# Moving two rank events, one exponential, the routing weights and the halves of a matrix product in the first stage of a transformer-and-experts kernel

## What is computed

```
q = (x @ Wq).reshape(B, L, H, d)
feat = elu(q) + 1.0
KV = einsum('nshd,nshv->nhdv', feat, q / L);  Ksum = feat.sum(axis=1)
Z = 1.0 / (einsum('nlhd,nhd->nlh', feat, Ksum) + 1e-6)
msg = einsum('nlhd,nhdv,nlh->nlhv', feat, KV, Z) * L
msg = msg.reshape(B, L, D) @ Wm
x1 = x + _layernorm(msg, g1, b1)
mlp = relu(msg @ W1) @ W2
x1 = x1 + _layernorm(mlp, g2, b2)
x1 = _layernorm(x + x1)
logits = x1 @ router_w.T
probs = softmax(logits);  topk_w, topk_ids = top_k(probs, 8)
topk_w = topk_w / topk_w.sum()
pos = rank of each token among those that chose the same expert
```

## Time and profile before

| | |
|---|---|
| median of 3 runs | 648.25 us (645.24 to 648.62) |
| profiled execution | 652.67 us |
| span of its trace | 650.7 us |
| PE busy | 562.6 us (86%) |
| DVE busy | 462.1 us (71%) |
| POOL busy | 427.9 us (66%) |
| ACT busy | 305.8 us (47%) |
| first stage, by PE | from 4 us to 137 us of the span |

### The profile page before, as it was taken

The page is one execution under the profiler, slowest core; times in us unless marked ns, Lnnn a source line. Parts: engine busy times, 40 slices in busy tenths (PEclk is TensorE's granted clock), DMA queues, the critical chain, the costliest instruction groups (busy, mean ns, idle before and its releaser), DMA issues.

```text
span 650.7 us, 10440 instructions
## 1 busy us (share of the span) xinstructions
PE 562.6 (86%) x3231; PEld 459.8 (71%) x3231; DVE 462.1 (71%) x1568; ACT 305.8 (47%) x825; POOL 427.9 (66%) x471
## 2 busy tenths in 40 slices
PE   5889888899238877999899999999999999999993
PEld 4678777855226655787687887878878788788762
DVE  1577877789949423576677879778787787886873
ACT  3667756449201111225364736636456365463440
POOL 5453422319574576538887988979979799753673
PEclk9999989799555555579999999999999999999998
DMA  4688455789320121142330030300302100000000
GB/s 130 170 229 316 186 218 196 313 255 233 80 73 28 47 61 50 37 170 99 127 131 2 8 138 9 135 4 10 138 9 93 46 9 9 2 17 0 10 8 17
DMA packets 47225, 62.04 MB, mean 95 GB/s; under 512 B 13026, under 2 KB 39873, under 8 KB 46146
## 3 DMA queue, kind: packets, MB, share of 16 engines
q1 hardware_dynamic: 44610, 56.15, 26.8%
q0 software_dynamic: 2560, 5.23, 2.8%
HBM read 35.16 MB, written 24.13 MB: 91 GB/s over the span
## 4 chain that ended last, share of the span: by engine, by line
PE 59%; DVE 19%; issue 6%; ACT 6%; POOL 3%; DMA 3%; another core or an unknown queue 2%; SPq 1%; POOLq 0%; DVEq 0%; ACTq 0%
PE pair L1446 8%; PE pair L1448 8%; PE pair L1447 8%; PE pair L1779 5%; DVE c_g L1247 2%; PE pair L602 2%; PE pair L628 2%; PE pair L1558 2%; DVE cand L1975 2%; PE pair L1494 2%; PE pair L1789 2%; PE pair L1568 2%; PE pair L555 2%; POOL c_acc L959 2%
## 5 line engine op out<-in xcount | busy, mean ns | idle before, releaser
L959 POOL TENSOR_TENSOR c_acc<-c_acc,c_g 128x512 f32<-128x512 f32 x112 | 144.6, 1291 | 37.6 <-DVE c_g L1247 30.0
L1095 ACT ACTIVATE c_sg<-pair 128x256 f32<-128x256 f32 x256 | 95.3, 385 | 93.3 <-PE pair L1448 90.4
L1247 DVE SCALAR_TENSOR_TENSOR c_g<-pair,c_comb,c_sg 128x256 f32<-128x256 f32 x224 | 100.4, 478 | 27.0 <-ACT c_sg L1095 22.7
L1446 PE MATMUL pair<-c_w_hi,c_x3h 128*128 128x512 f32 x256 | 108.9, 426 | 12.2 <-DVE c_g L1247 11.3
L1448 PE MATMUL pair<-c_w_hi,c_x3l 128*128 128x512 f32 x256 | 101.0, 395 | 0.0
L1447 PE MATMUL pair<-c_w_lo,c_x3h 128*128 128x512 f32 x256 | 100.7, 393 | 0.0
L1446 PEld LDWEIGHTS pair<-c_w_hi,c_x3h 128*128 128x128 f32 x256 | 48.2, 188 | 23.5 <-DVE c_g L1247 14.2
L1448 PEld LDWEIGHTS pair<-c_w_hi,c_x3l 128*128 128x128 f32 x256 | 48.0, 188 | 11.2
L1447 PEld LDWEIGHTS pair<-c_w_lo,c_x3h 128*128 128x128 f32 x256 | 48.3, 189 | 8.0
L1857 POOL DMA_INDIRECT routed_rows<-x1T_all,dest_row x32 | 31.7, 992 | 28.9 <-DVE x1T_all L1769 21.2
L1852 POOL DMA_INDIRECT rows_all<-token_rows,tok_row x32 | 31.3, 978 | 14.8 <-issue 9.4
(11 more groups left out here) (374 smaller groups left out, 1489.3 us busy)
## 6 DMA issues: line engine op xcount, KB each, us to landing
routed_rows<-rows_all SPq DMA_DIRECT2D x8, 2048.0 KB
c_c<-routed_rows SPq DMA_DIRECT2D x7, 2048.0 KB, 7.8
token_rows<-a_xw SPq DMA_DIRECT2D x8, 384.0 KB, 2.8
a_x<-in_L_attn_x SPq DMA_DIRECT2D x8, 256.0 KB, 3.0
base_all<-a_xw SPq DMA_DIRECT2D x8, 256.0 KB, 3.5
c_c<-routed_rows SPq DMA_DIRECT2D x4, 512.0 KB, 5.2
out<-c_outb SPq DMA_DIRECT2D x16, 128.0 KB, 1.8
wgu_late<-in_L_ffn_w_gate SPq DMA_DIRECT2D x4, 480.0 KB, 7.7
```

Of the source, the lines that this page charges most:

```text
L959: g.tensor_tensor(acc, acc, b["g"][:, (2 * uf + i) % 4, :, :], ALU.add).then_inc(s["acc"], 1)
L1095: a_.activation(b[f"sg{q % 2}"][:, x, :], self.pair[q % 2][:, x, H1:2 * H1], SIG).then_inc(s["sig"], 1)
L1247: v.scalar_tensor_tensor(out=dst, in0=self.pair[q % 2][:, x, 0:H1], scalar=b[f"comb{uf}"][:, j * E1 + e:j * E1 + e + 1], in1=b[f"sg{q % 2} ...
L1446: t.matmul(dst, w_hi, x_hi, start=start, stop=False)
```

## The change

1. **Events.** Events 0 and 1 both stand in step 7, the last sequence's step. Step 6 becomes a full step like those before it. To have both in one step, event 0 uses banks 1 and 2, event 1 uses banks 0 and 6, with new waits: the first half of `hT` in step 8 for both `keyT` writes, event 1's products for `msg_sb`, and the fillers of step 7 for both copies of `maskT`.
2. **Halves.** The first half of W1's product goes to bank 6, the second to bank 5. Only the second half waits for the copy of the logits.
3. **Exponential.** On ACT, L303 stands ahead of the copy of `msgT` in steps where the next q is made early.
4. **Routing weights.** On DVE, L509, L511 and L515 stand ahead of L497 to L504.
5. **Fillers.** 4 rather than 6 in a step; the 20 of step 9 stay.

```diff
-    EVENTS = {6: (0,), 7: (1,), B + 2: (2, 3)}
+    EVENTS = {7: (0, 1), B + 2: (2, 3)}
...
-                a.activation(b["hT"][:, 0, :], bank[5][:, :], ACT.Relu).then_inc(s["hT_sb"], 1)
+                a.activation(b["hT"][:, 0, :], bank[6][:, :], ACT.Relu).then_inc(s["hT_sb"], 1)
                 act.wait_ge(s["hT_mm"], 2 * n + 2)
-                a.activation(b["hT"][:, 1, :], bank[6][:, :], ACT.Relu).then_inc(s["hT_sb"], 1)
+                a.activation(b["hT"][:, 1, :], bank[5][:, :], ACT.Relu).then_inc(s["hT_sb"], 1)
...
-                a.copy(b["maskT"][:, i % 2, :], bank[0 if i == 3 else 1][:, :]).then_inc(s["maskT_sb"], 1)
+                a.copy(b["maskT"][:, i % 2, :], bank[1 - i % 2][:, :]).then_inc(s["maskT_sb"], 1)
...
+            if self.ahead(k + 1):
+                exponential(k + 1)
...
-                exponential(k + 1)
+                    exponential(k + 1)
...
-            if k < self.N and k in self.EVENTS:
-                self.write_keys(dve, self.EVENTS[k][0])
+            if k < self.N:
+                for i in self.EVENTS.get(k, ()):
+                    self.write_keys(dve, i)
...
                 pe.wait_ge(s["msgT_sb"], n + 1)
+                if n == self.N - 1:
+                    pe.wait_ge(s["key_sb"], 2)
...
-                if n >= 2:
-                    pe.wait_ge(s["lg_sb"], n - 1)
                 for h in range(2):
-                    t.matmul(bank[5 + h][:, :], b["WmW1"][:, h * D:(h + 1) * D], b["msgT"][:, :], start=True, stop=True).then_inc(s["hT_mm"], 1)
+                    if h and n >= 2:
+                        pe.wait_ge(s["lg_sb"], n - 1)
+                    t.matmul(bank[6 - h][:, :], b["WmW1"][:, h * D:(h + 1) * D], b["msgT"][:, :], start=True, stop=True).then_inc(s["hT_mm"], 1)
...
-                unread(20 if n == self.N - 1 else 6, bank[0])
+                if k in self.EVENTS and k < self.N:
+                    pe.wait_ge(s["maskT_sb"], 2)
+                unread(20 if n == self.N - 1 else 4, bank[0])
...
-                    pe.wait_ge(s["key_sb"], 1)
-                rank = bank[6 if i == 3 else 2]
+                    pe.wait_ge(s["msg_sb"], k + 1)
+                rank = bank[6 if i % 2 else 2]
```

More of the change, by code:

```diff
@@ L491, in dve @@
                 v.tensor_tensor(by_half(ex), by_half(ex), mask, ALU.mult).then_inc(s["pick"], 1)
+            if 0 <= m < self.N:
+                dve.wait_ge(s["pick"], 5 * m + 3)
+                v.tensor_reduce(b["esum"][:, :], ex, AX.X, ALU.add).then_inc(s["pick"], 1)
+                dve.wait_ge(s["pick"], 5 * m + 4)
+                v.reciprocal(b["esum"][:, :], b["esum"][:, :]).then_inc(s["pick"], 1)
+                dve.wait_ge(s["pick"], 5 * m + 5)
+                if m >= 2:
+                    dve.wait_ge(self.xw_stored[m % 2], 32 * (m // 2))
+                v.tensor_tensor(b[f"xw{m % 2}"][:, :, D:ROW], ex, bcast_last(b["esum"][:, :], E0), ALU.mult).then_inc(s["w_sb"], 1)
             n = k
@@ L506, in dve @@
                 ins.then_inc(s["msg_sb"], 1)
[L507 to L515, removed]
             n = k - 1
@@ L546, in write_keys @@
         at = h * 2 * L + part * L
-        v.scalar_tensor_tensor(out=self.keyT[:, at:at + L], in0=bank[6 if i == 3 else 2][:, :], scalar=b["offs"][:, part:part + 1],
+        v.scalar_tensor_tensor(out=self.keyT[:, at:at + L], in0=bank[6 if i % 2 else 2][:, :], scalar=b["offs"][:, part:part + 1],
                                in1=b["maskT"][:, h, :].bitcast(F32), op0=ALU.add, op1=ALU.mult).then_inc(s["key_sb"], 1)
@@ L636, in pe @@
                     pe.wait_ge(s["featT_sb"], k + 1)
-                transposes(bank[0 if i == 3 else 1], lambda j: b["mask"][:, part, j, h, :, :].rearrange("p u e -> p (u e)")).then_inc(s["maskT_mm"], 1)
+                transposes(bank[1 - i % 2], lambda j: b["mask"][:, part, j, h, :, :].rearrange("p u e -> p (u e)")).then_inc(s["maskT_mm"], 1)
             n = k
```

## The result

| | before | changed |
|---|---|---|
| median of 20 runs each, same chip | 649.61 us | 646.24 us |
| lowest and highest | 645.24, 653.08 us | 642.46, 650.08 us |
| ratio, 95% interval | | 0.9951 (0.9928 to 0.9973) |
| profiled execution, span | 652.67, 650.7 us | 650.08, 648.1 us |

The change is faster by 3.4 us (0.5%; 1.8 to 4.7 by the interval) where 5.45 (0.84%) was forecast. The time of 646.24 lies just inside the range of 640.8 to 646.5, but by size the forecast missed: taken from the median of 20 runs before, 649.61, it would have said 644.2. The profiled execution of the changed kernel took 650.08 us, the longest of its 20 runs. It shows well what can go wrong, and it is not a typical execution.

What follows compares the result with a forecast made beforehand. A chain across engines, no engine being full, was taken to set the step. Terms: -3.0 + 0.3 + 0 + 0 - 4.85 + 2.1 = -5.45 us, taking 648.25 to 642.8; range (8 in 10) 640.8 to 646.5.

Steps and rivals of the forecast that it cites:

- Turns: Ends of steps 2 to 5: W1's first half no longer waits for the logits' copy, 0.75 us each, -3.0 us.
- Early steps: Steps 0 and 1: the early exponential delays step 0's path; step 1's delay is covered by the feat wait; +0.3 us once.
- Fillers and weights: Full steps: two fillers less only lengthen PE's wait for x1; the weights fill DVE's wait for num; 0 us each.
- the 646.3 that has a chance of 0.04: Outcome in the prediction's spread of chances: 646.3 us, chance 0.04.
- Step 6: Becomes a full step without its event: 12.13 us instead of 16.98, -4.85 us.
- Step 7: Takes both events, with a 2.1 us wait for the mask copies: 14.4 us instead of 12.28, +2.1 us.
- the rival at 0.25: The clock falls in step 7's new wait: one fall costs 1.7 us, so -3.7 and 644.5 us; chance 0.25.
- The rest of the kernel: Stages behind the first, from keyT in step 10: assumed to let the whole gain through.
- The second rival: Median executions had no slow stretch in step 6: 1.7 us of gain missing, some tenths spilled; about 646.2 us; chance 0.12.
- the first rival: The clock falls in step 7's new wait, one fall costing 1.7 us: 644.5 us; chance 0.25.

Runs made afterwards that it cites:

- e4: Kernel before with only the halves of W1's product swapped and the logits' wait on the second half: 627.71 us, ratio 0.9904.
- e10: Changed kernel with 6 fillers in a step instead of 4: 643.95 us, ratio 0.9939 to the kernel before.
- e12: Kernel before with halves swapped, weights moved and exponential early from step 2; events in steps 6 and 7, 6 fillers: 643.30 us, ratio 0.9918.
- e3: Kernel before with both events in step 7, with their banks and waits, and nothing else: 634.06 us, ratio 1.0004.
- e7: Kernel before with only the routing weights moved ahead of z and msg on DVE: 632.17 us, ratio 0.9985.
- f3: Further profiled execution of the kernel before, nothing changed, on a third chip: 636.65 us.
- f4: Second further profiled execution of the kernel before, nothing changed, on a third chip: 632.41 us.
- e2: Changed kernel with eight more unread products ahead of step 7's wait for both maskT copies: 626.95 us, ratio 0.9883 to the kernel before.
- e1: Changed kernel timed once more, nothing altered, beside the kernel before: 632.00 us, ratio 0.9959.

## Why the forecast was right and where it was not

**Turns, -3.0 forecast.** Right in mechanism, a little small: 0.92 each, -3.7 for four. The halves alone give 0.85 (e4). The other 0.07 are the two fillers less: with six of them a full step takes 12.03 us in e10, and in e12 too, which has the early exponential. Beside the swapped halves the exponential adds nothing to a full step. I took 0.75, with an allowance of my own for a semaphore between, which no row shows; L607 starts 0.84 after L692, whose row takes 1.00, and 0.84 was the upper end.

**What the turns were also worth.** This was missing. e4 gave 6.6 us (4.4 to 7.9 by its interval), while the steps of its profile give about 5.0 against those of the kernel before without a fall: 3.4 in steps 2 to 5, 1.35 in step 6, 0.3 in step 7. With the wait at the turn went the falls behind it, one or two of 1.7 us in three of three profiled executions of the kernel before (none in those of e3 and e7, which have the same turns). That these falls are the missing 1.6 fits the sizes and was not tested by itself. I read one of them in the earlier trace rows and treated it as a matter of step 6.

**Early steps, +0.3.** 0.27 in step 0, and 0.27 in step 1 that the wait for `feat` covered (0.74 before, 0.47 after). The rest of the +1.24 in the table is not the change's: products between 14.6 and 16.3 us took twice their time, and the same stands in f3, an execution of the kernel before. Their cause stays open, since the granted clock reads 1.00 there. Of step 2's -1.72 some 0.5 is such a piece too: 14.37 with PE waiting 0.30 us for a load of x, 13.88 in other profiles of the kernel before.

**Fillers and weights, 0.** Nearly right: the fillers gave 0.07 in a full step, and the weights nothing there, with the 2.13 us of L530 as worked out. What they give in a step with an event (0.38, e7) the working did not see, and the changed kernel has no use for it. POOL went first in each full step, by 0.06 to 0.07 us (in step 4 L262 at 65.24, L532 at 65.31, to 67.44):

```profile
65.24 1.26 POOL L262 TENSOR_TENSOR a_r<-a_x,a_b 128x512 f32<-128x512 f32 x1
...
65.31 2.13 DVE L532 SCALAR_TENSOR_TENSOR a_r<-a_gm,a_rstd,a_r 128x128 f32<-128x128 f32 x4 [0.33 <-POOL a_rstd L254]
```

No run shows the 646.3 that has a chance of 0.04 in the prediction, a delay of POOL's addition by DVE's: the additions stood in this order in all full steps.

**Step 6, -4.85.** This term was mis-sized. It set a length of 16.98, with a fall in it, against one without. Without a fall step 6 took 15.29 (f4), so the term was -3.3 (15.29 to 11.96). Of that 1.35 comes from the halves alone (e4: 13.94), and 2.0 is left for the events' move. The working had said itself that 1.7 of the term hung on the fall. That this 1.7 was not missing in the end is luck: one or two such falls went with the waits at the turns, which the sum had not counted there.

**Step 7, +2.1.** Measured +2.06 (14.34) when the clock is kept, by the steps that were worked out: wait 1.91 for 2.1, end at 14.34 for 14.4. So beside the halves the events' move makes steps 6 and 7 longer by 0.34 us (11.96 + 14.34 against 13.94 + 12.02 in e4), a small loss. The two terms had booked a gain of 2.75.

**The clock in the new wait.** This is the step that failed. The term of step 7 let the clock stay up through a new wait of 2 us, so the sum had the fall at nothing, and the rival at 0.25 priced it at 1.7. Step 7 lost 3.25 (17.59 against 14.34) and step 8 to the end 1.3 more (26.90 against 25.6) in the profiled execution. e2 against e1 puts the filled wait at 5.05 us in the median. I had taken the length of a fall from the earlier trace rows, where it lasted for about one L602: that took 3.59 us, and from 82.5 to 86.1 us the mean granted clock was 0.53. Here it lasted 10 us. What is not shown is how many executions have this fall: none of the three profiles of the changed kernel on the faster chips does, and there the account rests on e2's median.

**The sum again.** Turns -3.7, start +0.3, step 6 -3.3, step 7 +2.1 give -4.6. One or two falls that the turns lose add -1.7 to -3.4: -6.3 to -8.0. The changed kernel with its wait filled (e2) measured -7.3 (5.6 to 9.2 by its interval), so without the fall in the new wait the gain is larger than the 5.45 of the forecast. That fall gives back the 5.05 of e2 against e1 and leaves -1.3 to -3.0. Measured were 2.3 (e1) and, on the first chip, 3.4.

**The rest of the kernel** let the gain through, as assumed, on the faster chip: 493.7 to 495.3 us from the first stage's end in eight kernels. In the six profiles from the slower sets it took 510.2 to 513.5 us, so there a part of every difference between single executions comes from behind the stage.

**The rivals' sums.** Two do not come out of their own terms. The second rival takes back 1.7 us and "some tenths", which makes 644.5 and a little more, not 646.2. The forecast's own range of 641.3 to 644.3 is wider than the bounds of its terms, which add up to about 642.1 to 643.8. That the measured 646.24 stands beside the 646.2 of the second rival and inside the range is chance: what happened is the first rival, at a higher price.

## What to carry to other kernels

Before a change is priced against a profile, its slow-clock stretches have to be taken out of the terms, or priced by their own: a fall in the one execution shown can be missing from the next (three profiles of the kernel before had theirs at the start of step 6, of steps 4 and 6, and of step 5). A new wait of PE can cost more than its own length: behind the one of 1.91 us the granted clock was 0.50 for 10 us in one profile of the changed kernel, and stayed at 1.00 in three others. If it can't be avoided, put work into the wait, which cost nothing on the path here (14.34 us with and without, e2 and e1); work behind it showed no gain (e10). And test a bundle part by part: here one part, the swap of two banks with its later wait (e4), was worth more than the whole (e1).

## What the runs showed of the hardware

The granted clock fell to 0.50 behind waits of only 0.68 and 0.72 us (before, f3, f4), and in steps 3 to 9 it stayed low between some 3.4 us (e10) and 10 us (the changed kernel), the latter with PE busy without a gap. A DVE instruction (L515) that started 0.16 us after POOL's addition did (L262, at 93.38 us in the kernel before) took 1.39 us, against 0.43 in step 4. The kernel before took 649.0 and 649.6 us in two sets and 632 to 634 us in the three others, which ran on other chips. Full steps had the same length on all of them (11.95 to 11.97 in the changed kernel), and the difference lies behind the first stage: about 512 us against 494.5. Its cause was not looked for.
